# Re-ordering both ends of a one-core token-mixer, attention and mixture-of-experts kernel

## The reference

```python
# tokens: 16-long patches with stride 8, real FFT, times W -> (8, 64*16, 64): 8192 tokens of 64
x_emb = concat(xf.real, xf.imag) @ W.T
# attention over all tokens: f = tokens / |tokens|
attn = softmax(f @ f.T);  att = attn @ f
h = layernorm(h + l2norm(0.8 * f + 0.2 * att))
# experts: top 2 of 8 by softmax of the router, weights renormalised
out = h + sum_e combine[:, e] * (gelu(h @ w1[e] + b1[e]) @ w2[e] + b2[e])
h = layernorm(h + out)
```

## Time and profile before

| | us |
|---|---|
| three runs | 893.47, 895.53, 896.09 (median 895.53) |
| the profiled execution, its own time | 891.0 |
| its span, first to last instruction | 889.2 |
| PE busy | 860.1 (97%) |
| DVE busy | 770.5 (87%) |
| ACT busy | 651.8 (73%) |
| GpSimd busy | 169.6 (19%) |

### The profile page before, as it was taken

How to read it: one execution, slowest core, us unless ns; L and a number is a source line. 1 busy time by engine, 2 the same in 40 slices (tenths; PEclk the granted TensorE clock), 3 DMA queues, 4 the chain that set the end, 5 groups by cost and what they waited for, 6 DMA issues and landing times.

```text
span 889.2 us, 30574 instructions
## 1 busy us (share of the span) xinstructions
PE 860.1 (97%) x13244; PEld 431.5 (49%) x13244; DVE 770.5 (87%) x924; ACT 651.8 (73%) x1271; POOL 169.6 (19%) x184
## 2 busy tenths in 40 slices
PE   4998999999999999999999999999999999999996
PEld 2444555555555555555555555555555555543331
DVE  5334999999999999989998998899889899988985
ACT  0124887888788878878787878787878787877764
POOL 4045500000120000000000000000000499946123
PEclk9999999999999999999999999999999999999998
DMA  9997410000000000000000000000000000000111
GB/s 273 230 275 127 72 38 3 3 2 3 3 3 2 3 3 2 3 3 2 3 3 3 2 2 3 2 3 3 3 3 2 3 2 2 3 1 14 24 25 36
DMA packets 28870, 26.46 MB, mean 30 GB/s; under 512 B 9568, under 2 KB 26464, under 8 KB 28736
## 3 DMA queue, kind: packets, MB, share of 16 engines
q1 hardware_dynamic: 19568, 14.98, 7.5%
q10 hardware_dynamic: 8752, 8.86, 3.9%
q0 software_dynamic: 416, 0.66, 0.4%
HBM read 18.21 MB, written 2.10 MB: 23 GB/s over the span
## 4 chain that ended last, share of the span: by engine, by line
PE 89%; DVE 4%; ACT 2%; DMA 2%; issue 2%; SPq 0%; POOL 0%; POOLq 0%; DVEq 0%; ACTq 0%
PE ps L455 37%; PE ps L472 26%; PE ps L485 12%; PE ps L388 6%; PE ps L541 2%; DMA ring<-in_x_dram 2%; PE ps L498 2%; DVE ring L1056 1%; ACT ring L774 1%; PE ps L611 1%; ACT ring L808 1%; PE ps L519 1%; PE ps L423 1%; DVE h L967 0%; DVE h L1062 0%
## 5 line engine op out<-in xcount | busy, mean ns | idle before, releaser
L914 DVE TENSOR_TENSOR ring<-ring 128x1024 f16<-128x1024 f32 x512 | 602.7, 1229 | 45.6 <-ACT ring L808 45.2
L808 ACT ACTIVATE ring<-ps 128x1024 f32<-128x1024 f32 x512 | 519.7, 1021 | 131.0 <-PE ps L455 130.7
L455 PE MATMUL ps<-big 64*64 64x512 f16 x6144 | 375.2, 376 | 2.2 <-ACT ring L808 2.0
L472 PE MATMUL ps<-ring,fs 64*64 64x512 bf16 x4096 | 274.4, 384 | 0.0
L455 PEld LDWEIGHTS ps<-big 64*64 64x64 f16 x6144 | 171.6, 106 | 164.6 <-ACT ring L808 5.1
L472 PEld LDWEIGHTS ps<-ring,fs 64*64 64x64 f16 x4096 | 116.1, 106 | 109.9
L485 PE MATMUL ps<-ring,fs 64*64 64x512 f16 x2048 | 153.5, 376 | 0.1
L808 ACT ACTIVATION_READ_ACCUMULATOR ring<-ps 128x1 f32 x512 | 101.4, 198 | 0.0
L335 POOL TENSOR_SCALAR stat<-stat 128x16 f32<-128x16 f32 (+2 forms) x4 | 1.9, 466 | 449.8 <-DVE stat L963 449.5
L485 PEld LDWEIGHTS ps<-ring,fs 64*64 64x64 f16 x2048 | 58.4, 107 | 52.8 <-PE ps L472 0.8
L388 PE MATMUL ps<-ring,weff 128*128 128x512 f32 x128 | 60.2, 627 | 7.3 <-DMA ring<-in_x_dram 6.9
(11 more groups left out here) (143 smaller groups left out, 457.2 us busy)
## 6 DMA issues: line engine op xcount, KB each, us to landing
ring<-in_x_dram ACTq DMA_DIRECT2D x8, 1024.0 KB, 15.0
ring<-in_x_dram SPq DMA_DIRECT2D x8, 1024.0 KB, 13.5
big<-big SPq DMA_DIRECT2D x16, 128.0 KB, 2.3
out_dram<-h SPq DMA_DIRECT2D x14, 128.0 KB, 2.4
f<-in_L_tok_W_dram SPq DMA_DIRECT2D x1, 288.0 KB, 4.0
fs<-consts_dram ACTq DMA_DIRECT2D x1, 256.0 KB, 22.2
xedge<-in_x_dram POOLq DMA_DIRECT2D x2, 128.0 KB, 7.2
w1s<-in_L_ffn_w_dram POOLq DMA_DIRECT2D x2, 128.0 KB, 7.5
```

Of the source, the lines that this page charges most:

```text
L455: last = mm(bank(SLOT_BANK[slot_of(s)] + r)[m:m + 64, :], of_k[r][:, 128 * k + m:128 * k + m + 64], of_q[r][:, q0 + 512 * r:q0 + 512 * r + ...
L472: last = mm(bank(sums_bank(s // NT) + half)[m:m + 64, :], fs[64 * r:64 * r + 64, s % NT, m:m + 64], probs[64 * r:64 * r + 64, s % 8, :].bi ...
L808: a(probs[:, s % 8, :], bank(SLOT_BANK[slot_of(s)], 2), ACT.Exp, accum_out=rowsum[:, s:s + 1]).then_inc(s_pr, 1)
L914: tt(probs_lo[:, s % 8, :], probs[:, s % 8, :], probs[:, s % 8, :].bitcast(BF16)[:, 1:2 * QC:2], ALU.subtract).then_inc(s_lo, 1)
```

## The change

It has these parts.

- `first_products` goes over the pairs (b, s) as (0,0) (0,1) (0,2) (1,0) (1,1) (1,2) (0,3) (1,3) instead of s by s. Matmuls whose result nobody reads (`kept_busy`, 128 x 128 float32 of the identity) stand ahead of them (14), behind (0,0) (4) and behind (0,1) (6).
- The eight loads of `w1`, the router, `w2` and `b1` move from GpSimd's queue to SP's, behind the last load of `x` and ahead of the first DMA transpose. GpSimd's loads of `xedge` and `b2` wait for batch 1 of `x` instead of `weff`.
- `scores(0)` moves ahead of the last two `tokens` on PE; the wait for all of DVE's `tokens_out` moves from pair 1 to pair 2. The late squares, highs and norms move to later steps.
- Tail: `token_transposes` and `transposed_out` move from quarter 3 to quarter 2, the `b2s` product from the last to the first quarter, `out_squares` and `final_variance` of groups 0 to 5 into the first quarter of the next group, `scaled` and `result_added` to quarter 3, and the 13 route steps split 4, 3, 6 instead of 3, 5, 5. The scaling of the variance (L985) moves from DVE to GpSimd.

```diff
-LATE_SQUARES = {2: 6, 3: 7}
-LATE_HIGHS = {4: 5, 14: 6, 22: 7}
-LATE_NORMS = {1: 6, 4: 7}
+BUSY_AHEAD, BUSY_BEHIND = 14, (4, 6)
+LATE_SQUARES = {10: 6, 16: 7}
+LATE_HIGHS = {12: 5, 22: 6, 30: 7}
+LATE_NORMS = {12: 6, 18: 7}
...
             # SyncE, behind the loop over x
+            sp.wait_ge(s_zero, 3)
+            for half in range(2):
+                rows = slice(64 * half, 64 * half + 64)
+                sp.dma_start(w1s[rows].rearrange("p (e k) -> p e k", e=E),
+                             w1.rearrange("e d k -> d e k")).then_inc(s_w, 16)
...
             # GpSimd
-            pool.wait_ge(s_zero, 3)
-            pool.wait_ge(s_weff, 1)
+            pool.wait_ge(s_xb[1], 16)
+            pool.wait_ge(s_xc[1], 16)
...
+                then(pool_ts(stat[:, VAR_OUT, t], stat[:, VAR_OUT, t], 1.0 / D, 1e-5, ALU.mult, ALU.add))
...
             # TensorE
+            def kept_busy(n):
+                for i in range(n):
+                    mm(bank(7)[:, 0:128], ident, ident, start=True, stop=True)
...
-                for s in range(HALF):
+                for b, s in ((0, 0), (0, 1), (0, 2), (1, 0), (1, 1), (1, 2), (0, 3), (1, 3)):
                     pe.wait_ge(s_weff, s + 1)
...
+                    if b == 0 and s < 2:
+                        kept_busy(BUSY_BEHIND[s])
...
+            kept_busy(BUSY_AHEAD)
             first_products()
...
+            pe.wait_ge(s_hilo[0], 16)
+            pe.wait_ge(s_lohi[0], 32)
+            pe.wait_ge(s_prodev, B - 1)
+            scores(0)
+            tokens(B - 2)
+            tokens(B - 1)
+            pe.wait_ge(s_prodev, B)
...
-                if c == 1:
-                    pe.wait_ge(s_h, NG)
...
+                if c == 2:
+                    pe.wait_ge(s_h, NG)
...
+                if i == 0:
+                    for n in range(2):
+                        mm(bank(4)[64 * n:64 * n + 64, :], b2s[:, n, :], combT[:, y % 2, :],
+                           start=True, stop=False, skip_group_check=True)
...
+                    if i == 2 and g + 2 < NG:
+                        token_transposes(g + 2)
                     if i == 3 and g + 1 < NG:
                         combine_transposes(g + 1)
-                    if i == 3 and g + 2 < NG:
-                        token_transposes(g + 2)
...
             # ScalarE
+                    if i == 2 and y < NG:
+                        transposed_out(y)
+                    if i == 3 and q < NG:
+                        combine_out(q)
+                    if i == 3 and z >= NG - 2:
                         for w in pieces_of(z):
                             out_squares(w)
+                    if i == 0 and 0 <= z - 1 < NG - 2:
+                        for w in pieces_of(z - 1):
+                            out_squares(w)
...
             # VectorE
-                then(red(stat[:, VAR_OUT, t], sq_o[:, 2 * p0:2 * p1, :], AX.X, ALU.add))
-                ts(stat[:, VAR_OUT, t], stat[:, VAR_OUT, t], 1.0 / D, 1e-5, ALU.mult, ALU.add).then_inc(s_var2, 1)
+                red(stat[:, VAR_OUT, t], sq_o[:, 2 * p0:2 * p1, :], AX.X, ALU.add).then_inc(s_var2, 1)
...
-            STEPS_OF = ((0, 1, 2), (3, 4, 5, 6, 7), (8, 9, 10, 11, 12), ())
+            STEPS_OF = ((0, 1, 2, 3), (4, 5, 6), (7, 8, 9, 10, 11, 12), ())
```

More of the change, by code:

```diff
@@ L259, in _ @@
                              x_h[b, 0]).then_inc(s_xb[b % XR], 16)
+            sp.wait_ge(s_zero, 3)
[3 more added lines that the diff above has]
+                             w1.rearrange("e d k -> d e k")).then_inc(s_w, 16)
+                with nc.allow_non_contiguous_dma(reason="512 floats"):
+                    sp.dma_start(routers[rows, E * half:E * half + E], router_w.rearrange("e d -> d e")).then_inc(s_w, 16)
+                sp.dma_start(w2s[rows], w2[half:E:2].rearrange("i k o -> k i o")).then_inc(s_w1r, 16)
+                with nc.allow_non_contiguous_dma(reason="512 floats"):
+                    sp.dma_start(b1s[rows], b1[half:E:2].rearrange("i k -> k i")).then_inc(s_w1r, 16)
             for i in range(NG):
@@ L393, in loaded @@
                 pe.wait_ge(s_xc[b % XR], 16 * (b // XR + 1))
+            def kept_busy(n):
+                for i in range(n):
+                    mm(bank(7)[:, 0:128], ident, ident, start=True, stop=True)
             def first_products():
-                for s in range(HALF):
+                for b, s in ((0, 0), (0, 1), (0, 2), (1, 0), (1, 1), (1, 2), (0, 3), (1, 3)):
                     pe.wait_ge(s_weff, s + 1)
[L398 to L404, removed]
+                    if s == 0:
+                        loaded(b)
+                    for q in range(2):
+                        last = product(b, q, s)
+                    if s == HALF - 1:
+                        last.then_inc(s_prod, 1)
+                    if b == 0 and s < 2:
+                        kept_busy(BUSY_BEHIND[s])
             def products(b):
@@ L609, in down @@
                 pe.wait_ge(s_hw, 2 * u + 2)
+                if i == 0:
+                    for n in range(2):
+                        mm(bank(4)[64 * n:64 * n + 64, :], b2s[:, n, :], combT[:, y % 2, :],
+                           start=True, stop=False, skip_group_check=True)
                 for n in range(2):
                     last = mm(bank(4)[64 * n:64 * n + 64, :], w2s[:, i, :], hidc[:, (2 * u + n) % 4, :],
[L612 to L616, removed]
+                              start=False, stop=(i == NPAIR - 1), skip_group_check=True)
                 last.then_inc(s_dn, 1)
@@ L1125, in _ @@
                         denominators(3)
-                    if i == 0 and y < NG:
+                    if i == 0 and g <= 1:
                         scaled(y)
@@ L1135, in _ @@
                             route(q, step)
+                    if i == 0 and 0 <= z - 1 < NG - 2:
+                        for w in pieces_of(z - 1):
+                            final_variance(w)
                     if i == 1 and y < NG:
                         normed(y)
-                    if i == 3 and z >= 0:
+                    if 0 <= z and i == (2 if z >= NG - 2 else 3):
+                        for w in pieces_of(z):
+                            result_added(w)
+                    if i == 3 and 1 <= g and y + 1 < NG:
+                        scaled(y + 1)
+                    if i == 3 and z >= NG - 2:
                         for w in pieces_of(z):
```

23 lines of the change are left out of this document (3 added, 20 removed).

## The result

The changed kernel takes 882.29 us (median of 4 runs, 881.89 to 882.67). The kernel before, on the same chip, took 894.77 (4 runs, 893.47 to 896.09). The ratio is 0.9874, with a 95% interval of 0.9859 to 0.9888: 12.5 faster. I had predicted 888.3, with a range from 885.0 to 892.0. The direction was right, the size was not.

What follows compares the result with a forecast made beforehand. PE was taken to bound the kernel, with DVE close behind in the tail. Gains of 3.2 (head), 0 (weights), 1.1 (transition), 3.0 (tail) and -0.1 (end) sum to 7.2; off the median 895.5: 888.3, range 885.0 to 892.0.

Steps and rivals of the forecast that it cites:

- Term 1: Head, first products: they end at 30.4 and not 33.6, 3.2 earlier, by fewer passes and a higher clock.
- rival D: Head: the keep-busy matmuls overrun at half clock and delay (0,2); whole gain 4.9, 890.6; chance 0.12.
- W: Time the moved weight loads take on SP's queue ahead of the first transpose: 3.9, with room for 5.0.
- rivals B and C: Weight loads on SP's queue cost more: B 10.7, 894.0, chance 0.07; C 14.9, slower at 898.2, chance 0.05.
- Term 2: From the products' end (P) to scores: pair 4 1.9 earlier, part given back to DVE, 1.1 left.
- Term 3: Tail: groups take 12.25 instead of 12.78, 3.0 gained, at most 4.5, PE's whole idle time.
- Rival A: Tail and middle: DVE stays the pace, PE's idle time only changes place; gain 4.2, 891.3; chance 0.20.

Runs made afterwards that it cites:

- e5: The kernel before with only the new order of the first products, no keep-busy matmuls: 888.16, ratio 0.9953.
- e7: The kernel before with only the tail's parts of the change, with the variance scaling on GpSimd: 889.09, ratio 0.9963.
- e8: The kernel before with only `scores(0)` early and the late squares, highs and norms at later steps: 891.57, ratio 0.9991.
- e6: The changed kernel with the weights and GpSimd's loads put back as before: 884.19, ratio 0.9908 to the kernel before.
- e1: The kernel before, unchanged, run and profiled again: 893.09, ratio 0.9981.
- e2: The kernel before with only keep-busy matmuls added (14 ahead of the first products, 12 behind (0,0)), old order: 893.32, ratio 0.9993.
- e3: The kernel before with only the eight weight loads moved to SP's queue and GpSimd's rest behind batch 1: 891.35, ratio 0.9965.
- e9: The kernel before with GpSimd's eleven loads kept on its own queue but held until batch 1 has landed: 890.11, ratio 0.9961.
- e4: The changed kernel without any keep-busy matmuls: 882.53, ratio 0.9870 to the kernel before.
- e11: The changed kernel with 7 instead of 14 keep-busy matmuls ahead: 883.02, ratio 0.9892 to the kernel before.
- e10: The changed kernel with the scaling of the variance back on DVE for the last three pieces: 881.26, ratio 0.9864 to the kernel before.
- e12: The changed kernel with both 7 keep-busy matmuls ahead and the last three variance scalings on DVE: 882.59, ratio 0.9878 to the kernel before.

## Why the prediction was wrong in its size, and where it was right

**The step that failed: "against the median of the runs, 895.5, it is 888.3".** The sum started from a profile in which batch 1 landed at 19.57. That landing was a draw, not a property of the kernel. In the seven profiled executions with GpSimd's loads issued from about 13.3 on, it came at 19.34 (e5), 19.57 (before), 20.45 (e7), 21.29 (e8), 22.52 (e6), 23.26 (e1) and 24.84 (e2). With these loads held it came at 18.99 (e3), 19.04 (e9), 19.11 (changed), 19.26 (e4), 20.43 (e11), 20.55 (e10) and 20.85 (e12). I had the evidence in sight: the profiled execution was 4.5 shorter than the median, and I carried the difference over as a constant. It is made in the head, and the new order takes PE's wait for it away. e1 shows the size, 3.5 for 3.7 of landing, and e2, 4.8 for 5.3; e5 shows the removal, 4.6 in the medians.

**The same step, in the other words of the prediction: "The loads of `xedge` and `b2` start some 6 and 2 us later ... I cost this at nothing."** Their own data were indeed never late. But their start, and the weights' with them, was not free for `x`: e9 gains 3.5 by the wait alone. The landings above show 1.9 of it (means of 21.6 and 19.7); what makes up the rest no trace shows.

**Term 1 (3.2 said).** Between the two profiles 2.73. The clock came out as said (1.00 from 20 to 24), the end at 30.87 and not 30.4. The cause is that of rival D at a smaller price: all 28 passes ahead ran at 0.213, to 14.90, and pushed (0,2) from 19.8 to 20.57. I had priced the whole overrun at 2.5; it was 0.8, since (0,0) and (0,1) then ran at the full clock. In the medians the term is larger by the lateness: 4.6. And the keep-busy matmuls, which I counted as its cover, are worth nothing here: without them (0,0) starts at 13.34 and partly at the low clock, and its products end at 30.34, a little earlier than 30.87:

```profile
13.34 17.00 PE ps L393 x32
```

The Trainium skill ("TensorE: Matmul & The Clock Gate", What's actually happening) says that activity releases the clock. The rows agree only in part: in the changed kernel 28 passes without a pause, and 72 ahead of them, all came at the low level, while in e10 the same 28 took 5.21 and in e2's timeline 4.67 (6.03 in the changed kernel's), so the pace rose among them; in e11 (0,0) stayed low to its end.

**The weights on SP's queue (W = 3.9, wait 0): right.** W was 4.3 and there was no wait; rivals B and C, with 10.7 and 14.9, fell. The 0.5 that is left of the room is less than the 1.1 that I had. The one price for all runs, 20.5 ns, fits only as a mean: the trace's packets of these loads, from 64 to 71, took 9 ns for 4 bytes and 27 for 256, 18 on average.

**Term 2 (1.1 said): 1.3.** Pair 4 came at P + 11.3 (said 11.2, before 13.1), which is 1.8. The number was met by another path than the one I stepped through: the chain to pair 4 runs over DVE (`tokens_out`, then four low parts), and PE waited 0.34 for DVE ahead of the low sums of pair 3, where I had only PE and ACT. The start of step 64's exponential, 168.38 before and 164.18 after, is 4.2 earlier, of the 2.89 + 1.8 = 4.7 of pair 4. So 0.5 was given back. It lies where the prediction had it, in pairs 13, 15 and 17, in which the low sums take 0.47, 0.56 and 0.68 of the chain and not 0.43:

```profile
114.35 0.47 PE ps L492 x8
...
119.66 0.56 PE ps L492 x8
...
125.04 0.05 issue
125.09 0.63 PE ps L492 x8
```

These low sums start 0.15 behind the end of the DVE low part that they wait for. The three delays are 0.4 in all, less than the 0.8 that I had taken off.

**Term 3 (3.0 said, cap 4.5): 4.95, and 0.7 lost at the end (0.1 said).** `up` behind `combine_transposes(1)` starts at 792.41 before and 788.27 after, the last such `up` at 868.52 and 859.43: 4.1 and 9.1 earlier. The cap was wrong, since it took the busy time of PE and DVE as fixed. The step that failed is "GpSimd's scaling beside DVE still stretches one instruction": in the three groups in which it had stretched `scaled` it now stretches none of DVE's (the mean of 1.259 became 0.683, in e7 too, with groups of 11.82), and there `normed` starts 0.07 ahead of GpSimd's scaling where `scaled` had started 0.13 behind it. The five groups are 4.55 shorter: PE's idle time fell by 3.5, and PE itself was busy for 1.1 less; records of matmuls can be missing and a group's edge has moved, so the 1.1 stays open. How much of the 3.5 is the spared DVE time, and how much the new places of the other instructions, isn't shown, since the tail's parts were only run together. At the end the three scalings on GpSimd (0.20, 0.20 and 0.43, with 0.08 of pause behind each) stood back to back with the roots, where I had counted two in the open. e10 gets this back. e7 agrees with both: 3.7 in the medians for 4.95 less the end's loss.

**The sum, made again.** Between the profiles: 2.73 + 0.16 (up to P, which moved by 2.89) + 1.3 + 4.95 - 0.7 = 8.4, which is what they show; the 0.7 is the remainder of 8.4 behind the 9.1. In the medians: 4.6 (order) + 1.9 (e6 to the changed kernel) + 1.2 + 3.7 = 11.4 of 12.5. That sum is rough: the 1.9 compares kernels timed on different occasions, and the kernel before has medians of 892.76 to 894.77 on four of them, so the rest can't be told from its own spread. Rival A (DVE stays the pace) fell with term 3.

What stays open is why the landing of batch 1 varies. Two parts can be told apart. Batch 0's own landing varied from 12.70 to 15.03 over all the profiles, and was late (14.45) in e12 too, with GpSimd's loads held; so a part arises without them. From batch 0's landing to batch 1's it took 6.6 to 9.8 with these loads beside it and 6.0 to 7.5 with them held; so they add to it. Whether by their packets or their descriptors was not tried. It is the half of each batch on SP's queue that varies: ACT's half of batch 1 landed between 16.8 and 18.8 in all 14 profiles.

## What to carry to other kernels

Where the profiled execution is faster than the median by as much as the change is worth, ask which wait varies before subtracting anything from the median: profile the kernel before a second time. Here a load that nobody needed for 20 us was best started behind the one that everybody waited for (3.5 in e9), on its own queue. And when two engines collide, ask of a moved instruction which of the two will start first at its new place, since in these traces the later one is stretched, and the busy time of the pace-setter is not a constant.

## What the runs showed that was not expected

- With loads of 0.66 MB issued on GpSimd's queue from about 13.3 on, beside the end of a 2 MB batch, that batch landed between 19.3 and 24.8 in seven profiles; with them held until it had landed, between 19.0 and 20.9 in seven others.
- In one execution PE ran 28 float32 passes at 0.213 each, without a pause and behind 72 others, with no rise to the full pace of 0.111; in that of e10 the same 28 took 5.21 and not 5.96. The four passes of (0,0), 128 x 512 each, took 1.72 behind 28 such passes and 3.48 behind 14 and a pause of 1.49.
- A GpSimd instruction on 128 x 512 floats beside a DVE one on the same kind of tile cost DVE 0.77 where GpSimd's started first (1.45 for 0.68), and itself 0.47 where DVE's did (1.51 for 1.04).
